# The masked cross-attention of a two-layer decoder, rewritten: strips, a ring of four, last keys a group ahead

## The chip, the cores and the metric

One core of one Trainium2 chip runs the whole program in one launch. The metric is the device time of that launch in microseconds (us), the median of several runs. The engines are PE (TensorE, matmuls; PEld its weight loads), DVE (VectorE), ACT (ScalarE), POOL (GpSimd) and SP (SyncE, which here only issues DMAs). Each takes its own instructions strictly in order and waits at semaphores for the others.

## What is computed

Six layers follow each other on x of 128 batches x 32 tokens x 256 features. The change lies in the first one, a cross-attention over 257 keys per batch with a mask:

```
x = x + L0_xattn(layernorm(x), ctx, ctx, mask, Wq, bq, Wk, bk, Wv, bv, Wo, bo)
   q, k, v: 16 heads of 16 features;  scores = q k^T / 4, masked keys at -1e9
   softmax over the 257 keys;  out = (probs v) Wo + bo
x = x + L0_attn(layernorm(x))      (state space)
x = x + L0_ffn(layernorm(x))       (quantised)
x = x + L1_xattn(layernorm(x), ctx, ctx)   (sigmoid in place of softmax, no mask)
x = x + L1_attn(layernorm(x));  x = x + L1_ffn(layernorm(x))   (experts)
```

## The kernel before, in words

Each layer is a function that is run to its end before the next starts. `cross_attention(..., layer=0)` makes the first; `soft` is true there. Nearly every product is made of three fp16 matmuls: an operand is kept as a high part (`kh`, `vh`, `pTh`, ...), which ACT rounds out of the fp32 result in PSUM, and a low part (`kl`, `vl`, `pTl`), which DVE gets by subtracting; `split_products` pairs high*high, high*low and low*high.

The work is cut into 128 batches, four to a group (128 tokens) and eight to a pass of the hardware loop. Each engine has its `body(i)` with a fixed order of steps for `c` in 0 to 7, written out by hand; nothing else sets the order. For batch b:

- PE: `keys` (12 matmuls of 256 columns into `psK`), `values` (12 into `psV`), `scores`: one product for each four of the 16 heads, 3 matmuls of 128 rows, 12 in all, into `psS`; right behind them the scores of the 257th key, 12 matmuls of one column, into `psSx`. Zeros in `qbd` (the queries spread to 8 heads of 32 tokens, others masked by `mask8`) keep heads apart. Two batches later `transposes` (8, fp32) turns the probabilities into `psT`, and `pv` multiplies them with the values into `psO`.
- DVE: `softmax_max` adds the mask to the 257th score (L842), then adds the mask to the scores and takes the row maximum, one instruction for each four heads (L847), then scales the maxima to the exponent's bias `nm` (L850). `recip` makes 1/sum. `lo_k`, `lo_v`, `lo_pT` make low parts. `extract` picks, out of `psO`, each head's own rows: one step on ACT and three on DVE (L907) for each pair of batches.
- ACT: `hi_k`, `hi_v`, `hi_pT`, and `probs`: four exponentials with their sums (L709), when `nm` is there.
- POOL: `split` makes the two parts of the context; `spread` builds `qbd` (four instructions of 1024 elements a group, L360); `norm` multiplies the probabilities with 1/sum, four instructions a batch (L380), and copies the 257th into `px`. PE's `transposes` wait for that (`p_norm`).
- Once a group, at `c % 4` = 0 to 3, `psA`, a part of the PSUM tile `psM`, is used in turn for the transposed x (`xnT`), the queries, the 257th keys and values (`row257`, with DVE's `lo_257` at L817 and L819 and `mask_257` at L826), and the output product. `psX` and `psSx`, other parts of `psM`, take the transposed 257th probabilities and the 257th scores.

K, `prob` and the maxima have two buffers, `pTh`/`pTl` one, V four. The fourth layer's `sigmoid_attention` (x1), which stays as it is, does a like job without softmax: four buffers for K, V and pT, keys two batches ahead, and matmuls that use parts of the array: two of 64 rows side by side in its `scores` (L1247), four of 32 columns side by side in its `attend` (L1267).

Of the kernel before, what the change touches and what calls it, by code (L numbers as in the profile page):

```python
# [180 lines left out]
def cross_attention(nc, d, xres, con, norm, layer):  # L181

    soft = layer == 0
    with ExitStack() as ctx:
# [1 line left out]
        sb, ps, sem = sp.sb, sp.ps, sp.sem  # L190
# [18 lines left out]
        V = [(sb(f"vh{n}", [P, C, 256], F16), sb(f"vl{n}", [P, C, 256], F16)) for n in range(4)]
        kx = [(sb(f"kxh{n}", [P, C, GB], F16), sb(f"kxl{n}", [P, C, GB], F16)) for n in range(2)]  # L210
        xk = (sb("xkh", [P, C, 96], F16), sb("xkl", [P, C, 96], F16))
        vx3 = sb("vx3", [96, D], F16)
        vxm = [sb(f"vxm{n}", [96, GB, D], F16) for n in range(2)]

        NP = 2
        prob = [sb(f"prob{n}", [P, 4, S2], F32) for n in range(NP)]
        pT32 = sb("pT32", [P, 4 * 256], F32) if not soft else None
        mx = [sb(f"mx{n}", [P, 4], F32) for n in range(2)]
        nm = [sb(f"nm{n}", [P, 4], F32) for n in range(2)]
        sm = [sb(f"sm{n}", [P, 4], F32) for n in range(2)]  # L220
        rs = [sb(f"rs{n}", [P, 4], F32) for n in range(2)]
        pT = [(sb(f"pTh{n}", [P, 2, 512], F16), sb(f"pTl{n}", [P, 2, 512], F16)) for n in range(1 if soft else 2)]
# [9 lines left out]
        psA = psM[:, 0:256]
        psX = psM[0:96, 256:384]
        psKx = psM[:, 384:392]
        psSx = psM[:, 392:408]
        score = [psS, psS] if soft else [psS, psT]
        SC = 0.25 / (WS * WS)
        PXS = 1.0 if soft else PS

        const_in, bias_ready, px_zeroed = sem("const_in"), sem("bias_ready"), sem("px_zeroed")  # L240
        ctx_in = [sem(f"ctx_in{n}") for n in range(2)]
        mask_in, mask_used = sem("mask_in"), sem("mask_used")
        pool_passed, sync_passed = sem("pool_passed"), sem("sync_passed")
# [3011 lines left out]
```

## Time and profile before

| | us |
|---|---|
| median of 3 runs | 3246.75 (3215.63 to 3252.71) |
| the profiled execution's own time | 3239.74 |
| its span, first to last instruction | 3237.9 |
| PE busy | 2671.7 (83%) |
| DVE busy | 2315.1 (71%) |
| ACT busy | 1925.8 (59%) |
| POOL busy | 1795.2 (55%) |

The median lies 7.0 us, 0.2%, above the profiled execution. The shares are means over six layers with different limits; the changed layer has the first 1130 us or so, and is to be read for itself. A busy engine is one with an instruction in it, and matmuls overlap, so what a matmul costs PE is the distance to the next start, not its duration.

### The profile page before, as it was taken

The page shows a single profiled execution, that of the slowest core. Times are in us where ns is not written, and L with a number is a line of the kernel's source. Part 1 is how long each engine was busy: PE and PEld are TensorE (multiplying, and loading weights), DVE is VectorE, ACT ScalarE, POOL GpSimd, SP SyncE. Part 2 cuts the span into 40 slices and gives each one's busy share as a digit, 9 for nine tenths or more (in the row PEclk, how much of TensorE's full clock was granted, in tenths as well). Part 3 has the DMA queues.
Part 4 walks back from the last instruction along what each step waited for, and adds up shares of the span by engine and source line. Part 5 has one row for each costly group of instructions (what it writes and reads, how often), then busy time and mean ns, then how long its engine had stood idle before and what let it go on. Part 6 is the DMA issues. An engine that isn't in the chain of part 4 may idle for free. (4 is left out here: it accounts for less than half of the span.)

```text
span 3237.9 us, 98846 instructions
## 1 busy us (share of the span) xinstructions
PE 2671.7 (83%) x35900; PEld 2137.6 (66%) x35901; DVE 2315.1 (71%) x5097; ACT 1925.8 (59%) x4544; POOL 1795.2 (55%) x2064
## 2 busy tenths in 40 slices
PE   3988888898888739999859699999994878537998
PEld 2777677777766627777635488888883667435776
DVE  4998899999888748888843577777775888563343
ACT  2666566666665548888724477777773656243333
POOL 4776777787776434555410466666662777133222
PEclk9999999999999859999979899999996999558999
DMA  4111111111110000000000222211110000351110
GB/s 142 41 59 41 44 56 49 48 59 39 42 59 28 14 1 1 1 0 0 1 28 1 77 60 70 61 58 58 59 44 16 2 2 2 133 193 49 36 34 28
DMA packets 87222, 140.66 MB, mean 43 GB/s; under 512 B 11040, under 2 KB 74304, under 8 KB 80736
## 3 DMA queue, kind: packets, MB, share of 16 engines
q1 hardware_dynamic: 82336, 123.04, 12.2%
q0 software_dynamic: 4672, 14.57, 1.3%
q8 instruction: 159, 2.61, 0.3%
q14 instruction: 55, 0.45, 0.0%
HBM read 122.88 MB, written 14.69 MB: 42 GB/s over the span
## 5 line engine op out<-in xcount | busy, mean ns | idle before, releaser
L380 POOL TENSOR_SCALAR x_prob<-x_prob,x_rs 128x257 f32<-128x257 f32 x512 | 246.8, 482 | 216.9 <-DVE x_rs L856 184.7
L709 ACT ACTIVATE x_prob<-x_prob,x_nm 128x257 f32<-128x257 f32 x512 | 254.4, 498 | 179.7 <-DVE x_nm L850 179.6
L2134 DVE TENSOR_TENSOR_SCAN m_s<-m_a,m_psBx 128x2048 f32<-128x2048 f32 x64 | 282.5, 4415 | 16.2 <-PE m_psBx L1909 15.7
L1425 DVE SCALAR_TENSOR_TENSOR x_pTl<-x_psS,x_pTh 128x1024 f16<-128x1024 f32 x128 | 156.8, 1225 | 168.0 <-ACT x_pTh L1333 168.0
L1920 PE MATMUL m_psS<-m_s,all_ident 128*128 128x256 f32 x1024 | 237.4, 386 | 0.9 <-DVE m_s L2134 0.9
L847 DVE CUSTOM_DVE_ANT_0 x_prob<-x_psS,x_masked,x_prob 128x256 f32<-128x256 f32 x512 | 217.5, 481 | 22.1 <-DVE x_prob L842 21.6
L1920 PEld LDWEIGHTS m_psS<-m_s,all_ident 128*128 128x128 f32 x1024 | 190.6, 191 | 45.8 <-issue 21.4
L2041 ACT ACTIVATE m_a<-m_dt,m_rate 128x248 f32<-128x248 f32 x512 | 205.6, 490 | 4.4 <-DVE m_s L2134 4.2
L3039 ACT ACTIVATE e1t_g<-e1t_psH,e1t_bias 128x128 f32<-128x128 f32 x312 | 88.9, 368 | 183.6 <-PE e1t_psH L2988 183.6
L693 ACT ACTIVATE x_kh<-x_psK,x_bk 128x256 f16<-128x256 f32 x256 | 107.3, 470 | 132.8 <-PE x_psK L265 130.2
L468 PE MATMUL x_psT<-all_ident,x_prob 128*128 128x128 f32 x1024 | 141.5, 282 | 52.4 <-issue 31.1
L865 DVE TENSOR_TENSOR x_pTl<-x_psT,x_pTh 128x512 f16<-128x512 f32 x256 | 164.1, 682 | 5.6 <-ACT x_pTh L680 2.9
L1114 POOL TENSOR_TENSOR x_qbdh<-x_qh,all_mask4h 128x1024 f16<-128x1024 f16 x32 | 60.6, 1893 | 176.7 <-DVE x_ql L1406 176.7
L468 PEld LDWEIGHTS x_psT<-all_ident,x_prob 128*128 128x128 f32 x1024 | 117.6, 145 | 58.6 <-issue 52.5
L1106 POOL TENSOR_TENSOR x_ctxl<-x_ctx,x_ctxh 128x512 f16<-128x512 f32 x128 | 148.6, 1161 | 10.7
L2988 PE MATMUL e1t_psH<-e1t_xnh,e_wh 128*128 128x128 f16 x624 | 143.4, 230 | 8.0 <-issue 7.5
L352 POOL TENSOR_TENSOR x_ctxl<-x_ctx,x_ctxh 128x512 f16<-128x512 f32 x128 | 143.4, 1120 | 10.7
L265 PE MATMUL x_psS<-x_kh,x_qbdh 128*128 128x256 f16 x512 | 142.4, 278 | 7.1 <-POOL x_qbdl L360 3.6
L1153 PE MATMUL x_psK<-x_ctxh,x_wkh 128*128 128x256 f16 x512 | 141.4, 276 | 4.7 <-POOL x_ctxl L1106 3.4
L1346 ACT ACTIVATE x_vh<-x_psV 128x512 f16<-128x512 f32 x128 | 76.4, 597 | 114.5 <-PE x_psV L1153 114.5
L265 PE MATMUL x_psV<-x_wvh,x_ctxh 128*128 128x256 f16 x512 | 143.4, 280 | 0.0
L265 PE MATMUL x_psV<-x_wvl,x_ctxh 128*128 128x256 f16 x512 | 143.2, 280 | 0.0
(554 smaller groups left out, 11481.1 us busy)
## 6 DMA issues: line engine op xcount, KB each, us to landing
x_ctx<-in_ctxT SPq DMA_DIRECT2D x32, 1028.0 KB, 5.3
x_ctx<-in_ctxT SPq DMA_DIRECT2D x32, 1024.0 KB, 6.0
x_mraw<-in_mask SPq DMA_DIRECT2D x128, 128.5 KB, 2.6
e1r_stage<-in_L_ffn_w SPq DMA_DIRECT2D x16, 1024.0 KB, 5.0
e_rows<-e1r_pad POOLq DMA_DIRECT2D x1, 5070.0 KB, 20.6
e1t_row<-e_rows SPq DMA_DIRECT2D x39, 130.0 KB, 2.1
all_xres<-in_x SPq DMA_DIRECT2D x1, 4096.0 KB, 14.4
x_vxr<-x_vx SPq DMA_DIRECT2D x128, 32.0 KB, 3.3
```

The source lines that it names most:

```text
L265: last = eng.matmul(out, a, b, start=start and n == 0, stop=stop and n == len(prods) - 1, skip_group_check=lint)
L352: pool.tensor_tensor(lo[:, j], src, hi[:, j], ALU.subtract).then_inc(ctx_split, 1)
L380: last = pool.tensor_scalar(prob[n][:, h, :], prob[n][:, h, :], rs[n][:, h:h + 1], PS, ALU.mult, ALU.mult)
L468: last = pe.transpose(psT[:, kt * 512 + h * P:kt * 512 + (h + 1) * P], prob[c % 2][:, h, kt * P:(kt + 1) * P], con["ident"][:])
L709: last = act.activation(prob[n][:, h, :], prob[n][:, h, :], ACT.Exp, bias=nm[n][:, h:h + 1], scale=SC, accum_out=sm[n][:, h:h + 1])
L847: dve.tensor_tensor_reduce(prob[n][:, h, 0:256], psS[:, h * 256:(h + 1) * 256], masked[gp][:, j, 0:256], 1.0, prob[n][:, h, 256:257], ALU. ...
L865: dve.tensor_tensor(pT[0][1][:, kt, :], psT[:, kt * 512:(kt + 1) * 512], pT[0][0][:, kt, :], ALU.subtract).then_inc(pt_lo, 1)
L1106: pool.tensor_tensor(lo[:, j], src, hi[:, j], ALU.subtract).then_inc(ctx_split, 1)
L1425: dve.scalar_tensor_tensor(pT[c % 4][1][:].rearrange("p r k n -> p (r k n)"), psS[c % 2][:], PS, pT[c % 4][0][:].rearrange("p r k n -> p ( ...
L1920: last = pe.matmul(psS[:, h * ST:(h + 1) * ST], con["ident"][:], S[h][:, :, m, :], start=m == 0, stop=m == NS - 1)
L2041: last = act.activation(A[h][:, :, m, 1:T], dt[c % 2][:, h, :].rearrange("p (b t) -> p b t", t=T)[:, :, 1:T], ACT.Exp, scale=rate[:, h, m: ...
L2134: dve.tensor_tensor_scan(rows(S), rows(A), psBx[:], 0.0, ALU.mult, ALU.add).then_inc(scan_done, 1)
```

## The change

`softmax_attention` takes the place of `cross_attention`; the other five layers are the same code.

- **Strips.** `scores` uses 64 rows of the array for four heads and the other 64 for the next four: per half 3 products, each as two matmuls side by side, into two different banks of `psS`. `qbd` is spread to 4 heads, not 8 (two POOL instructions a group). `attend` uses four strips of 32 columns side by side, 64 columns of data each.
- **Unnormalised weights.** POOL's `norm` is gone. The exponentials go straight to `transposes` (which wait for `exp_done`); the factor 4096 is applied where ACT and DVE take them out of `psT`. 1/sum is spread by POOL into `rsel` (`spread_sums`, 128 elements), turned to the layout of the output by two fp32 matmuls into `psR` (`attend_last`), and multiplied in by DVE's `extract`, now two steps on DVE.
- **The scale in the maximum.** L791 multiplies by `-SC` and takes the minimum, so that its result is the exponent's bias, and `probs` waits for each of the four results by itself.
- **A ring of four** for `prob`, `low` and K; two for pT. Keys two batches ahead, values one ahead; transposes one batch behind, attend two behind.
- **Last keys.** Keys and values of the 257th row for all 128 batches are made once at the start; the values go out to DRAM and come back in three copies for each group. Its scores are made for a whole group, a group ahead (`last_scores`, 24 matmuls of two columns), taken by DVE in one instruction (`take_scores`) and put into `prob` by POOL (`put_score`).
- **Order.** Each engine's `body` is new.

What it comes to on two engines, in the middle of a loop pass. DVE before, from one batch's low values to the next (L847: mask and maximum, its rows that repeat left out; `kxl` and `vx3` are the 257th row's, `oT` the output's own rows):

```order
L842 TENSOR_TENSOR x0_prob1<-x0_psM,x0_masked1 128x4 [waits x0_s_mm,x0_t_mm]
L847 ISA x0_prob1,x0_mx1<-x0_psS,x0_masked1,x0_prob1 128x256 [waits x0_sx_taken]
...
L850 TENSOR_SCALAR x0_nm1<-x0_mx1 128x4 [waits x0_s_max]
...
L886 SCALAR_TENSOR_TENSOR x0_kl0<-x0_psK,x0_bk,x0_kh0 128x256 [waits x0_s_mm,x0_k_hi]
...
L907 SCALAR_TENSOR_TENSOR x0_oT0<-x0_psO,all_mask4,x0_oT0 128x128 [waits x0_o_part]
...
L856 RECIPROCAL x0_rs1<-x0_sm1 128x4 [waits x0_p_main,x0_exp_done]
L817 SCALAR_TENSOR_TENSOR x0_kxl0<-x0_psM,x0_bk,x0_kxh0 128x4 [waits x0_vx_hi]
...
L819 TENSOR_TENSOR x0_vx3<-x0_psM,x0_vx3 32x256
...
L865 TENSOR_TENSOR x0_pTl0<-x0_psT,x0_pTh0 128x512 [waits x0_pv_mm,x0_pt_hi]
...
L894 TENSOR_TENSOR x0_vl2<-x0_psV,x0_vh2 128x512 [waits x0_pv_mm,x0_v_hi]
```

DVE now, the batch of a group in which most group steps fall (`obl`, `sxl`, once a group):

```order
L835 SCALAR_TENSOR_TENSOR x0_oT1<-x0_psO,all_mask2,x0_oT1 128x2x64 [waits x0_o_part]
L837 TENSOR_TENSOR x0_oT1<-x0_psO,x0_oT1 128x2x64 [waits x0_o_sum]
L791 ISA x0_prob2,x0_low2<-x0_psS,x0_masked0,x0_prob2 128x256 [waits x0_s_mm,x0_sx_put]
...
L820 SCALAR_TENSOR_TENSOR x0_kl0<-x0_psK,x0_bk,x0_kh0 128x256 [waits x0_s_mm,x0_k_hi]
...
L806 SCALAR_TENSOR_TENSOR x0_pTl1<-x0_psT,x0_pTh1 128x512 [waits x0_pv_mm,x0_pt_hi]
...
L798 RECIPROCAL x0_rs1<-x0_sm1 128x4 [waits x0_r_spread,x0_exp_done]
...
L843 SCALAR_TENSOR_TENSOR x0_obl0<-x0_oT1,x0_bv,x0_obh0 128x128 [waits x0_ob_hi]
...
L780 SCALAR_TENSOR_TENSOR x0_sxl1<-x0_psM,x0_barred1 128x16 [waits x0_sx_put]
L812 SCALAR_TENSOR_TENSOR x0_px3<-x0_psM,x0_px3 32x128 [waits x0_px_hi]
L828 TENSOR_TENSOR x0_vl3<-x0_psV,x0_vh3 128x512 [waits x0_pv_mm,x0_v_hi]
```

The 257th score's step and the scaling of the maxima have gone, `extract` stands ahead of the maxima and has one step less, the 257th row's `kxl` and `vx3` are replaced by one `sxl` for the whole group, and the low parts of the keys are those of two batches on.

PE before, the first matmul of each step of one batch (`psK` keys, `psT` transposes, `psV` values, `psS` scores, `psM` the 257th key's scores, `psO` the product with the values):

```order
L468 MATMUL x0_psT<-all_ident,x0_prob0 128x128 [waits x0_pt_lo,x0_p_norm]
...
L265 MATMUL x0_psV<-x0_wvh,x0_ctxh1 128x256 [waits x0_v_lo]
...
L265 MATMUL x0_psS<-x0_kh0,x0_qbdh1 128x256 [waits x0_s_max,x0_k_lo]
...
L265 MATMUL x0_psM<-x0_kxh1,x0_qbdh1 128x1 [waits x0_sx_taken]
...
L265 MATMUL x0_psK<-x0_ctxh1,x0_wkh 128x256 [waits x0_k_lo,x0_ctx_split]
...
L265 MATMUL x0_psO<-x0_pTh0,x0_vh0 64x128 [waits x0_pt_lo,x0_o_ext,x0_v_lo]
```

PE now, the same:

```order
L548 MATMUL x0_psS<-x0_kh1,x0_qbdh1 128x256 [waits x0_s_max,x0_k_lo]
...
L432 MATMUL x0_psK<-x0_ctxh1,x0_wkh 128x256 [waits x0_k_lo,x0_ctx_split]
...
L558 MATMUL x0_psT<-all_ident,x0_prob0 128x128 [waits x0_pt_lo,x0_exp_done]
...
L432 MATMUL x0_psV<-x0_wvh,x0_ctxh1 128x256 [waits x0_v_lo,x0_px_lo]
...
L574 MATMUL x0_psO<-x0_pTh1,x0_vh3 32x64 [waits x0_pt_lo,x0_v_lo]
...
L590 MATMUL x0_psO<-x0_px3,x0_vxm0 32x64 [waits x0_r_spread,x0_vxm_ready,x0_px_lo]
```

The transposes have moved from the head of the batch to behind the scores and the keys and wait for the exponentials, not for POOL; the single-column matmuls are gone from each batch; the last product now waits for POOL's `spread_sums` too.

The core of the diff (the order of each `body` is what the rows above show; DVE's and PE's lag by batch is as under **A ring of four**):

```
+            def put_score(i, c):
+                b, j, gp = i * 8 + c, c % GB, c // 4
+                wait_apart(pool, sx_taken, i * 2 + (gp + 1), pool_passed)
+                wait_apart(pool, t_mm, b - 3, pool_passed)
+                wait_apart(pool, px_put, b - 3, pool_passed)
+                pool.tensor_copy(prob[c % 4][:, :, LAST], sxl[gp][:, j, :]).then_inc(sx_put, 1)
...
-                    wait_apart(pool, r_ready, b + 1, pool_passed)
-                    for h in range(4):
-                        last = pool.tensor_scalar(prob[n][:, h, :], prob[n][:, h, :], rs[n][:, h:h + 1], PS,
-                                                  ALU.mult, ALU.mult)
-                    last.then_inc(p_main, 1)
...
+            def put_last(i, c):
+                b, j = i * 8 + c, c % GB
+                wait_apart(pool, exp_done, b * 4 + 4, pool_passed)
+                wait_apart(pool, pxT_mm, i * 4 + (c // 2 - 1), pool_passed)
+                dst = px[j // 2][:].rearrange("p (r z) -> p r z", r=3)[:, :, 4 * j:4 * j + 4]
+                pool.tensor_copy(dst, prob[c % 4][:, :, LAST].unsqueeze(1).to_broadcast([P, 3, 4])).then_inc(px_put, 1)
+
+            def spread_sums(i, c):
+                b, pair = i * 8 + c, c // 2 % 2
+                pool.wait_ge(r_ready, b + 1)
+                wait(pool, o_full, i * 4 + (c // 2 - 1))
+                pool.tensor_tensor(rsel[pair][:, c % 2], rs[c % 2][:].unsqueeze(2).to_broadcast([P, 4, T]),
+                                   token[:].unsqueeze(1).to_broadcast([P, 4, T]), ALU.mult).then_inc(r_spread, 1)
...
+            def last_scores(i, gp):
+                g = i * 2 + gp
+                pe.wait_ge(qbd_ready, g * 2 + 2)
+                for j in range(GB):
+                    for half in range(C):
...
+                wait(pe, s_max, b * 4)
+                for half in range(C):
+                    for m, (q, k) in enumerate(((0, 0), (0, 1), (1, 0))):
+                        for r in range(RG):
+                            rows = slice(64 * r, 64 * r + 64)
+                            to = r * 512 + half * LAST
+                            last = pe.matmul(psS[:, to:to + LAST], qbd[gp][q][rows, half, j].rearrange("p h q -> p (h q)"),
+                                             K[c % 4][k][rows, half, :], start=m == 0, stop=m == 2)
+                last.then_inc(s_mm, 1)
...
+                        to = (half * 2 + j % 2) * 64
+                        for v, p in ((0, 0), (0, 1), (1, 0)):
+                            for cg in range(4):
+                                frm = (half * 2 + cg // 2) * P + cg % 2 * 64
+                                last = pe.matmul(psO[32 * cg:32 * cg + 32, to:to + 64],
+                                                 V[c % 4][v][:, kt, half * P + 32 * cg:half * P + 32 * cg + 32],
+                                                 pT[c % 2][p][:, kt, frm:frm + 64],
+                                                 start=j % 2 == 0 and kt == 0 and half == 0 and (v, p) == (0, 0), stop=False,
...
+                for r in range(RG):
+                    last = pe.matmul(psR[64 * r:64 * r + 64].rearrange("p (c j t) -> p c j t", c=C, t=T), head_rows[:],
+                                     rsel[j0 // 2][:].rearrange("p j (c r) t -> p r c j t", c=C)[:, r],
+                                     start=True, stop=True, skip_group_check=True)
                 last.then_inc(o_full, 1)
...
+            def probs(i, c):
+                b = i * 8 + c
+                for h in range(4):
+                    act.wait_ge(s_max, b * 4 + h + 1)
+                    if h == 0:
+                        wait(act, r_ready, b - 1)
+                    act.activation(prob[c % 4][:, h, :], prob[c % 4][:, h, :], ACT.Exp, bias=low[c % 4][:, h:h + 1],
+                                   scale=-1.0, accum_out=sm[c % 2][:, h:h + 1]).then_inc(exp_done, 1)
...
-                wait_apart(dve, sx_taken, b + 1, dve_passed)
+                    wait_apart(dve, mask_used, i * 2 + (gp + 1), dve_passed)
                 for h in range(4):
-                    dve.tensor_tensor_reduce(prob[n][:, h, 0:256], psS[:, h * 256:(h + 1) * 256], masked[gp][:, j, 0:256],
-                                             1.0, prob[n][:, h, 256:257], ALU.add, ALU.max, mx[n][:, h:h + 1]).then_inc(s_max, 1)
-                dve.wait_ge(s_max, b * 4 + 4)
-                dve.tensor_scalar(nm[n][:], mx[n][:], -SC, None, ALU.mult).then_inc(nm_ready, 1)
+                    to = (h % 2) * 512 + (h // 2) * LAST
+                    dve.tensor_tensor_reduce(prob[c % 4][:, h, 0:LAST], psS[:, to:to + LAST], masked[gp][:, j, 0:LAST],
+                                             -SC, prob[c % 4][:, h, LAST:S2], ALU.add, ALU.min, low[c % 4][:, h:h + 1]).then_inc(s_max, 1)
...
+                dve.wait_ge(o_part, q + 1)
+                dve.scalar_tensor_tensor(dst, own_cols(1), con["mask2"][:, 1:2], dst, ALU.mult, ALU.add).then_inc(o_sum, 1)
+                dve.wait_ge(o_sum, q + 1)
+                dve.tensor_tensor(dst, psR.rearrange("p (c j t) -> p c j t", c=C, t=T), dst, ALU.mult).then_inc(o_ext, 1)
```

## Rows read from the trace of the kernel before

**Rows 1.** Busy time of each engine in three stretches (us, busy, instructions); clock, DMA.

```profile
300.00:600.00 300.00, 263.84 (x3374) 221.38 (x3373) 266.62 (x760) 192.72 (x598) 226.76 (x340) 0.98 0.17 53
...
1150.00:1200.00 50.00, 20.59 (x114) 14.08 (x114) 13.85 (x26) 21.14 (x39) 15.38 (x14) 0.57 0.00 0
...
2000.00:2400.00 400.00, 399.60 (x8694) 326.08 (x8692) 285.45 (x460) 300.63 (x480) 269.96 (x230) 1.00 0.21 62
```

**Rows 2.** Line L842, once a batch: min/median/max ns, first and last start.

```profile
L842 DVE TENSOR_TENSOR x_prob<-x_psM,x_masked x128: 145/154/167, 59.3 to 1108.6; 128x4 f32<-128x4 f32 x128
```

**Rows 3.** DVE's groups, 300 to 600 us: busy us, mean ns, idle before.

```profile
L847 DVE CUSTOM_DVE_ANT_0 x_prob<-x_psS,x_masked,x_prob 128x256 f32<-128x256 f32 x148 | 62.9, 481 | 7.1 <-DVE x_prob L842 7.1
...
L850 DVE TENSOR_SCALAR x_nm<-x_mx 128x4 f32<-128x4 f32 x37 | 35.1, 950 | 1.3
...
L907 DVE SCALAR_TENSOR_TENSOR x_oT<-x_psO,all_mask,x_oT 128x128 f32<-128x128 f32 x54 | 18.7, 346 | 1.3
...
L826 DVE TENSOR_TENSOR x_vxm<-x_vx,all_vmask 96x1024 f16<-96x1024 f16 x9 | 6.1, 677 | 0.0
L842 DVE TENSOR_TENSOR x_prob<-x_psM,x_masked 128x4 f32<-128x4 f32 x37 | 5.7, 154 | 1.4 <-PE x_psM L265 1.4
...
L819 DVE TENSOR_TENSOR x_vx<-x_psM,x_vx 32x256 f16<-32x256 f32 x9 | 3.7, 417 | 0.1
...
L817 DVE SCALAR_TENSOR_TENSOR x_kxl<-x_psM,x_bk,x_kxh 128x4 f16<-128x4 f32 x18 | 3.2, 218 | 3.5 <-ACT x_vx L673 3.5
```

**Rows 4.** The longest waits, 300 to 600 us: total, times, longest.

```profile
ACT x_prob L709 <- DVE x_nm L850: 55.7, 36, 2.2
POOL x_prob L380 <- DVE x_rs L856: 44.2, 23, 7.2
```

**Rows 5.** Line L850 over the layer.

```profile
L850 DVE TENSOR_SCALAR x_nm<-x_mx x128: 169/590/1616, 61.2 to 1110.5; 128x4 f32<-128x4 f32 x128
```

**Rows 6.** The order of time around one L850: start, us, engine.

```profile
604.96 3.75 POOL L360 TENSOR_TENSOR x_qbdl<-x_ql,all_mask 128x1024 f16<-128x1024 f16 x2
...
607.28 1.45 DVE L850 TENSOR_SCALAR x_nm<-x_mx 128x4 f32<-128x4 f32 x1
```

**Rows 7.** The order of time, PE matmuls of this layer.

```profile
603.68 0.16 PE L265 MATMUL x_psM<-x_kxl,x_qbdh 128*128 128x1 f16 x1
...
603.70 0.16 PE L265 MATMUL x_psM<-x_kxh,x_qbdl 128*128 128x1 f16 x1
...
603.73 0.27 PE L265 MATMUL x_psK<-x_ctxh,x_wkh 128*128 128x256 f16 x1
...
603.84 0.27 PE L265 MATMUL x_psK<-x_ctxl,x_wkh 128*128 128x256 f16 x1
...
605.32 0.23 PE L265 MATMUL x_psO<-x_pTh,x_vh 128*64 128x128 f16 x2
...
605.38 0.23 PE L265 MATMUL x_psO<-x_pTl,x_vh 128*64 128x128 f16 x2
```

**Rows 8.** The order of time, PE matmuls of the fourth layer, x1.

```profile
2102.01 0.20 PE L1267 MATMUL x_psO<-x_pTh,x_vl 128*32 128x64 f16 x4
2102.03 0.20 PE L1267 MATMUL x_psO<-x_pTh,x_vh 128*32 128x64 f16 x4
...
2104.57 0.22 PE L1247 MATMUL x_psS<-x_qbdl,x_kh 64*128 64x128 f16 x2
2104.63 0.22 PE L1247 MATMUL x_psS<-x_qbdh,x_kl 64*128 64x128 f16 x2
2104.78 0.28 PE L1153 MATMUL x_psK<-x_ctxh,x_wkh 128*128 128x256 f16 x1
```

**Rows 9.** POOL's costliest group, 300 to 600 us.

```profile
L380 POOL TENSOR_SCALAR x_prob<-x_prob,x_rs 128x257 f32<-128x257 f32 x148 | 71.3, 482 | 53.7 <-DVE x_rs L856 44.2
```

**Rows 10.** Two groups of layer x1, 2000 to 2400 us.

```profile
L1124 POOL TENSOR_TENSOR x_vxm<-x_vxr,x_own_head 64x1024 f16<-64x1024 f16 x21 | 45.5, 2166 | 0.0
...
L1451 DVE SCALAR_TENSOR_TENSOR x_obl<-x_oT,x_obh 128x256 f16<-128x256 f32 x20 | 12.7, 633 | 0.0
```

More of the change, by code:

```diff
@@ L209, in cross_attention @@
[L209 to L222, printed above, removed]
+        last32 = sb("last32", [P, C, NB], F32)
+        (lastp,), (kxp,), (kx,) = parts("last", [P, C, NB], 1), parts("kxp", [P, C, NB], 1), parts("kx", [P, C, NB, RG], 1)
@@ L232, in cross_attention @@
[L232 to L243, printed above, removed]
@@ L259, in cross_attention @@
         block = ctx.enter_context(nc.Block())
-        def mm_split(eng, out, lhs, rhs, start, stop, lint=False):
-            prods = [p for a, b in zip(lhs, rhs) for p in split_products(a, b)]
-            for n, (a, b) in enumerate(prods):
-                last = eng.matmul(out, a, b, start=start and n == 0, stop=stop and n == len(prods) - 1,
-                                  skip_group_check=lint)
-            return last
-        def both(pair, f):
-            return (f(pair[0]), f(pair[1]))
@@ L426, in _, with products, part @@
             run(pool, body)
-            norm(LASTI, 8)
+            spread_sums(LASTI, 6)
+            put_last(LASTI, 7)
+            spread_sums(LASTI, 7)
         @block.tensor
         def _(pe):
+            def products(out, lhs, rhs):
+                prods = [p for a, b in zip(lhs, rhs) for p in split_products(a, b)]
+                for m, (a, b) in enumerate(prods):
+                    last = pe.matmul(out, a, b, start=m == 0, stop=m == len(prods) - 1)
+                return last
+            def part(pair, f):
+                return (f(pair[0]), f(pair[1]))
@@ new lines, in keys @@
+            def keys(i, c):
+                b, j, gp = i * 8 + c, c % GB, c // 4
+                pe.wait_ge(ctx_split, b + 1)
+                if isinstance(i, int) and b == 0:
+                    pe.wait_ge(kx_lo, 1)
+                wait(pe, k_lo, b)
+                for h in range(C):
+                    last = products(psK[:, h * LAST:(h + 1) * LAST],
+                                    [part(W["k"], lambda w: w[:, cc, h * P:(h + 1) * P]) for cc in range(C)],
+                                    [part(ctxp[gp], lambda x: x[:, j, cc, :]) for cc in range(C)])
+                last.then_inc(k_mm, 1)
@@ new lines, in values @@
+            def values(i, c):
+                b, j, gp = i * 8 + c, c % GB, c // 4
+                if isinstance(i, int) and b == 0:
+                    pe.wait_ge(vx_lo, 1)
+                wait(pe, v_lo, b)
+                for kt in range(2):
+                    last = products(psV[:, kt * D:(kt + 1) * D],
+                                    [part(ctxp[gp], lambda x: x[:, j, cc, kt * P:(kt + 1) * P]) for cc in range(C)],
+                                    [part(W["v"], lambda w: w[:, cc, :]) for cc in range(C)])
+                last.then_inc(v_mm, 1)
@@ L647, in _ @@
+            transposes(LASTI, 7)
+            turn_taken(LASTI, 7)
+            turn_last(LASTI, 8)
+            attend(LASTI, 6)
+            attend(LASTI, 7)
+            attend_last(LASTI, 7)
             output(LASTI, 1)
@@ L779, in _ @@
+            hi_px(LASTI, 8)
+            extract(LASTI, 6)
             hi_ob(LASTI, 1)
```

864 lines of the change are left out of this document (396 added, 468 removed).

## The prediction

> **What bounds the kernel now.** I read the windows first, to get the layer by itself, then the line that runs once a batch, for the pitch, and then groups, waits and the order of time inside the layer. The changed layer gives a batch every (1108.6 - 59.3)/127 = 8.262 us [rows 2]; that pitch, 127 times, is what the change works on. From 300 to 600 us, 148 maxima of four a batch make 37 batches, one in 8.11 us [rows 3]. Divided by 37, the busy times there are PE 7.13, DVE 7.21, ACT 5.21, POOL 6.13 us a batch [rows 1]. So two engines are near the pitch at once, and each lacks about 0.9 to 1.0 us of being full. The waits say how that is lost: ACT waits 55.7 us for `nm`, and POOL 44.2 us for 1/sum [rows 4]. These lie on one loop: maxima on DVE, exponentials on ACT, 1/sum on DVE, scaling on POOL, transposes on PE, low parts on DVE again, with two buffers for `prob` and one for pT. ACT and POOL have slack; they are links of that loop, not limits by their own work. Neither PE nor DVE can be made faster alone.
>
> **PE, part by part**, by starts. A matmul of 256 columns starts 0.11 us after the last (603.73 to 603.84), one of a single column 0.025 (two between 603.68 and 603.73), a pair of the product with the values 0.06 [rows 7]. In layer x1 two matmuls of 64 rows and 128 columns start as a pair each 0.06 us, half of 0.11 for half the columns, so the second strip is free; and four strips of 32 columns and 64 data columns start each 0.03 us (2102.01 to 2102.03) [rows 8].
> - Scores: 12 x 0.11 = 1.32 before, 6 pairs x 0.11 = 0.66 now: -0.66.
> - Product with the values: 12 pairs x 0.057 = 0.68 before, 12 fours x 0.03 = 0.36 now: -0.32.
> - Single-column scores: 12 x 0.025 = 0.30 a batch before; 24 of two columns a group, 0.15 a batch: -0.15.
> - 257th keys and values once a group, 12 narrow and 6 wide matmuls, 0.30 + 0.66 = 0.96, /4: -0.24. They are made once at the start.
> - `attend_last`: 4 fours and two fp32 matmuls of 128 columns a pair of batches, in place of four of 128 columns (4 x 0.06). The fp32 ones cost between 0.1 and 0.3 us each; I take 0.2, so 0.12 + 0.4 - 0.24 = 0.28 a pair, +0.14.
> - Changes between whole and split array: in x1 the first whole matmul starts 0.15 us after the last pair (2104.63 to 2104.78), 0.09 more than the pitch [rows 8]. Scores go in and out once a batch: +0.18. The product with the values had its strips before.
> Sum: 7.13 - 0.66 - 0.32 - 0.15 - 0.24 + 0.14 + 0.18 = **6.08 us of PE a batch**. Keys, values and transposes are untouched and are most of it.
>
> **DVE.** Gone: `nm` 0.950; the 257th score 0.154; of three `extract` steps a pair one, 0.346/2 = 0.17; `mask_257` 0.677/4 = 0.17; `vx3` 0.417/4 = 0.10; `kxl` 2 x 0.218/4 = 0.11 [rows 3]. New: `sxl`, like the 0.154 row, 0.04; `lo_ob` now in two halves, each reading two SBUF tensors. The maxima still pitch as before (same shape, 481 ns). The nearest row to `lo_ob` is x1's 633 ns for both halves at once [rows 10]; two halves cost between that and twice it, against one instruction of about 0.42 (`vx3`, same columns): +0.05 to +0.21, I take 0.12. Sum: 7.21 - 1.65 + 0.16 = **5.72**.
>
> **ACT and POOL.** ACT loses the 257th row and half of `hi_ob`; it stays under its 5.21. POOL loses four scalings, 4 x 0.482 = 1.93 [rows 9], and two of four `spread` instructions of 3.75/2 = 1.88 each [rows 6], 0.94 a batch. It gains `own_rows`, near x1's 2.166, 0.54 a batch [rows 10], two small steps a batch of not over 0.2 each beyond the copy it had, and `spread_sums`, an eighth of a `spread` instruction, 0.25. Sum 6.13 - 1.93 - 0.94 + 0.54 + 0.65 = 4.4. Both lie well under PE. They cost nothing as work, but are links: what waits behind them is named under the rivals.
>
> **What is late next.** PE has the most work, 6.08, DVE 5.72 right under it. Of the loop, the links over POOL's scaling (four instructions, 1.9 us) and over `nm` are out; the first exponential may start after the first maximum. I walked one batch through the new orders, with t = 0 at DVE's first maximum of batch b. The maxima end at 1.65 and PE's scores of b+1 start (the one-deep `psS` waits for them). Keys of b+3 end about 3.9. The exponentials of b end near 2.2, low parts of b-1 near 3.9, so the transposes of b start without a wait. Values of b+2 follow by 5.7, when DVE's low values of b+1 are just done. The product of b-1 needs `extract`, the first thing in DVE's next turn. It fits, but with margins of some tenths only at `values`, `extract` and `psS`. DVE's turns are uneven: the one at `c % 4` = 0 carries the mask conversion and the queries. So I take 0.4 us of wait a batch on PE. Below it lies layer x1, same ring and lags, in which PE is busy 399.6 of 400 us, no wait [rows 1]; above it the 0.98 us of today. Pitch 6.08 + 0.42 = **6.50**.
>
> **The sum.** 127 x (8.262 - 6.50) = 223.8 us less. Start and end: four more constants are loaded ahead of the first context, the 257th rows of all batches go through PE once, and at the end one softmax tail without POOL's scaling; I take them together at 0, within 8 us either way. 3239.74 - 223.8 = 3016; the median shown lies 7 us above the profiled execution, so **3023 us**. What a measurement of this kernel can tell from no change is about 2%, 65 us, so faster means a pitch under about 7.75.
>
> **A rule against the trace.** L850 writes 4 numbers a row and takes 169 ns at best, 950 on the mean of the stretch [rows 3, 5]. In the order of time it starts at 607.28 and ends at 608.73, and POOL's `spread`, begun at 604.96, ends at 608.71 [rows 6]. So 0.78 of the 0.95 us taken off DVE above is waiting for POOL. The question is if the wait goes, or falls on DVE's next instruction.
>
> The Trainium skill, SBUF — State Buffer, "Who interferes with whom", says that DVE and GpSimd share a port pair as an exclusive lock, and that of DVE's instructions only 2-port forms such as `tensor_scalar`, and those with two SBUF inputs while GpSimd reads, are shut out. By this rule the wait goes with L850, since what follows reads PSUM; but `lo_ob` now has two SBUF inputs, twice a group. The trace agrees as far as it goes: x1's L1451, of that kind, has 633 ns.
>
> **Rivals.**
> 1. *No waits, as in x1.* For it: the same ring, and room on DVE. Against: x1 has no maximum and no transposes. Pitch 6.1 to 6.2: 3239.74 + 7 - 127 x 2.11 = 2979.
> 2. *The loop holds.* Today's 0.98 us of wait stays: `put_score` of a group waits for `take_scores`, which DVE does only behind `lo_ob` in the third batch; POOL's `spread` and `own_rows` delay `put_last`, for which PE's turn of `px` waits, and `spread_sums`, for which `attend_last` waits with the next scores and keys queued behind. Pitch 7.06: 3239.74 + 7 - 152.7 = 3094.
> 3. *The wait for POOL moves on.* 0.78 us falls on another DVE instruction: DVE 6.50, with 0.4 of waits 6.9: 3239.74 + 7 - 173 = 3074. POOL works less (4.4 for 6.13), which speaks against the whole of it.
> 4. *The strips do not run side by side here*, so that the change does not do what it says: scores 12 x 0.11 and the product with the values 48 x 0.03 = 1.44 cost 0.66 + 1.08 more, PE 7.82, pitch 8.2: 3239, no change. Rows of x1 speak against it.
> 5. *Slower: the clock.* Granted clock is 0.98 while PE is busy 264 of 300 us, and 0.57 while it is busy 20.6 of 50 [rows 1]. If the new waits let it fall to the lower of its levels (1.2 GHz) inside the layer, PE's 6.08 doubles to 12.2: 3247 + 127 x 3.9 = 3742. It decides from a mean clock under 6.08/8.26 = 0.74. But PE would be busy 6.08 of 6.5, more than today.
>
> **Chances.** Forecast (pitch 6.25 to 6.8) 0.50; rival 1 0.16; rivals 2 and 3 together 0.26, of which 0.02 beyond 7.75; rival 4 0.05; rival 5 0.03. That makes faster 0.90, within 2% 0.07, slower 0.03. The range has to take in rivals 1 to 3 with start and end: from 2979 less 8, rounded down to cover a cheaper `attend_last` (0.1 us a batch, 13 us), to 3094 plus 8 and a little for POOL's part: 2960 to 3115. Outside lie rivals 4 and 5 and the thin ends.
>
> **What the profile after would show.** Right: a pitch of 6.5; PE busy some 6.1 us a batch and over 90% of the layer, clock 0.98; score matmuls in pairs at 0.11 us; DVE near 5.7; the waits for `nm` and 1/sum gone, ACT idle for PE's keys and values. Wrong, by step: pairs at twice that start distance (rival 4); PE waiting on `px_put`, `r_spread` or DVE on `sx_put` for over 0.5 us a batch (rival 2); DVE rows such as the maxima or `lo_ob` longer than before (rival 3). The forecast fails most easily where my 0.4 us of wait is off, as it is a choice between rows, each 0.1 us being 13 us of the total.

## The result, and the profile after

The changed kernel takes 3121.8 us (median of 4 runs, 3112.6 to 3149.0) against 3237.6 in the same session, a ratio of 0.9675 [0.9593, 0.9757]. The forecast was 3023, the range 2960 to 3115. Line L791 has the maxima now, four a batch: the first at 58.1, the last at 944.0 us, so a pitch (the time from one batch to the next) of 885.9/127 = 6.98 us (before 8.262 [rows 2]; forecast 6.50).

Busy time of each engine in the profile after, as in [rows 1]; the short stretches are one passage between two passes of the layer's loop:

```profile
300.00:600.00 300.00, 268.08 (x4780) 222.27 (x4778) 241.81 (x744) 208.32 (x644) 180.01 (x268) 0.95 0.20 59
...
326.00:328.00 2.00, 2.00 (x77) 1.64 (x75) 2.00 (x6) 2.00 (x9) 2.00 (x3) 1.00 0.23 39
328.00:330.00 2.00, 0.45 (x15) 0.20 (x4) 1.23 (x3) 1.26 (x5) 1.92 (x4) 1.00 1.00 342
330.00:332.00 2.00, 0.00 (x0) 0.00 (x0) 0.29 (x1) 0.00 (x0) 2.00 (x7) 1.00 0.47 152
332.00:334.00 2.00, 0.10 (x2) 0.11 (x4) 0.00 (x0) 0.00 (x0) 1.68 (x2) 0.78 0.00 0
334.00:336.00 2.00, 2.00 (x16) 1.17 (x15) 0.12 (x1) 0.00 (x0) 0.00 (x0) 0.50 0.03 8
336.00:338.00 2.00, 2.00 (x11) 1.51 (x10) 1.58 (x8) 0.00 (x0) 0.00 (x0) 0.50 0.00 0
338.00:340.00 2.00, 2.00 (x13) 1.93 (x12) 0.87 (x2) 0.98 (x3) 0.00 (x0) 0.51 0.00 0
340.00:342.00 2.00, 2.00 (x34) 1.68 (x35) 1.42 (x3) 2.00 (x7) 0.00 (x0) 1.00 0.00 0
```

The first stretch holds 42 batches (x167 of L791): PE 6.38, DVE 5.76 busy a batch, pitch 7.14, where 6.08, 5.72 and 6.50 were forecast. The short ones show where it goes: TensorE stands for over 5 us, then works for 6 us at a granted clock of 0.50 (334 to 340 us), the lower of its two levels (1.2 GHz). The waits after, whole run for the first two, 300 to 600 us for the rest:

```profile
PE x_psS L548 <- issue: 69.0, 13, 5.5
PE x_psS L1190 <- issue: 34.1, 6, 5.7
...
ACT x_kh L680 <- PE x_psK L432: 82.9, 43, 8.9
POOL x_prob L350 <- DVE x_sxl L780: 56.1, 10, 5.6
POOL x_rsel L388 <- DVE x_rs L798: 45.9, 11, 8.6
...
DVE x_prob L791 <- PE x_psS L548: 27.4, 5, 5.6
...
ACT x_prob L664 <- DVE x_low L791: 7.0, 10, 0.8
```

Of the waits of [rows 4], ACT's for the bias has shrunk from 55.7 to 7.0 us. POOL still waits for 1/sum, 45.9 us for 44.2, but now with `spread_sums`, and no wait of TensorE for `rsel` appears in this stretch. At the top is a wait whose releaser is "issue": no semaphore explains it. It comes 13 times, each time before the first score matmul of a pass, and the layer's loop jumps back 13 times (of its 16 passes, the first and the last are written out, 14 are in the loop). In x1, whose code the change leaves alone, it comes 6 times. The order of time on PE around one of them:

```profile
328.01 0.44 PE L594 MATMUL x_psO<-x_rsel,x_head_rows 128*64 128x128 f32 x4
333.90 0.40 PE L548 MATMUL x_psS<-x_kh,x_qbdh 64*128 64x256 f16 x2 [5.45 <-issue]
334.08 0.42 PE L548 MATMUL x_psS<-x_kl,x_qbdh 64*128 64x256 f16 x2
```

Two more rows are of the kernel before, the same waits in the whole run and x1's line L1425; the last is the latter's counterpart after, L1368:

```profile
PE x_psT L468 <- issue: 31.1, 10, 4.7
...
L1425 DVE SCALAR_TENSOR_TENSOR x_pTl<-x_psS,x_pTh x128: 1223/1225/1226, 1835.0 to 2440.4; 128x1024 f16<-128x1024 f32 x128
```

```profile
L1368 DVE SCALAR_TENSOR_TENSOR x_pTl<-x_psS,x_pTh x128: 1223/1225/1226, 1663.6 to 2316.0; 128x1024 f16<-128x1024 f32 x128
```

x1 took 605.4 us and takes 652.4. From here on "x0" and "x1" are the times from first to last start of DVE's `x_pTl` in the two layers; x0 fell from 1041.4 to 878.9 (69.3 to 948.2), 162 us, of which x1 gives 47 back. They and the stalls are those of the one profiled execution of each kernel, the times in the tables the medians of all.

### The profile page after: what moved, and what is told of

The parts are those of the page before. It is cut to its first block and busy times, and to the rows that moved or that the text cites. A ratio compares the mean times of both kernels' runs of the same rounds, so it can differ in the third digit from the quotient of the medians.

```text
span 3122.1 us, 105389 instructions
## 1 busy us (share of the span) xinstructions
PE 2561.8 (82%) x38670; PEld 2034.0 (65%) x38671; DVE 2130.9 (68%) x4719; ACT 1878.5 (60%) x4388; POOL 1542.9 (49%) x1680
## 5 line engine op out<-in xcount | busy, mean ns | idle before, releaser
L1368 DVE SCALAR_TENSOR_TENSOR x_pTl<-x_psS,x_pTh 128x1024 f16<-128x1024 f32 x128 | 156.8, 1225 | 206.8 <-ACT x_pTh L1276 206.8
L791 DVE CUSTOM_DVE_ANT_0 x_prob<-x_psS,x_masked,x_prob 128x256 f32<-128x256 f32 x512 | 216.6, 478 | 73.5 <-PE x_psS L548 71.7
L664 ACT ACTIVATE x_prob<-x_prob,x_low 128x257 f32<-128x257 f32 x512 | 253.5, 503 | 20.6 <-DVE x_low L791 20.6
L806 DVE SCALAR_TENSOR_TENSOR x_pTl<-x_psT,x_pTh 128x512 f16<-128x512 f32 x256 | 163.5, 679 | 4.9 <-ACT x_pTh L672 4.0
L1270 ACT ACTIVATE x_psS<-x_psS 128x1024 f32<-128x1024 f32 x128 | 129.0, 1008 | 59.7 <-PE x_psS L1190 57.3
L1049 POOL TENSOR_TENSOR x_ctxl<-x_ctx,x_ctxh 128x512 f16<-128x512 f32 x128 | 149.5, 1168 | 10.7
L337 POOL TENSOR_TENSOR x_ctxl<-x_ctx,x_ctxh 128x512 f16<-128x512 f32 x128 | 148.9, 1163 | 10.7
L432 PE MATMUL x_psK<-x_ctxh,x_wkh 128*128 128x256 f16 x512 | 148.3, 290 | 5.8 <-POOL x_ctxl L337 3.4
L1096 PE MATMUL x_psK<-x_ctxh,x_wkh 128*128 128x256 f16 x512 | 144.3, 282 | 4.5 <-POOL x_ctxl L1049 3.0
L432 PE MATMUL x_psK<-x_ctxh,x_wkl 128*128 128x256 f16 x512 | 147.8, 289 | 0.0
L432 PE MATMUL x_psK<-x_ctxl,x_wkh 128*128 128x256 f16 x512 | 147.8, 289 | 0.0
L672 ACT ACTIVATE x_pTh<-x_psT 128x512 f16<-128x512 f32 x256 | 138.9, 594 | 12.0 <-PE x_psT L558 9.2
L1096 PE MATMUL x_psK<-x_ctxl,x_wkh 128*128 128x256 f16 x512 | 143.3, 280 | 0.0
```

The costliest lines, as they stand in the source:

```text
L337: pool.tensor_tensor(lo[:, j], src, hi[:, j], ALU.subtract).then_inc(ctx_split, 1)
L432: last = pe.matmul(out, a, b, start=m == 0, stop=m == len(prods) - 1)
L664: act.activation(prob[c % 4][:, h, :], prob[c % 4][:, h, :], ACT.Exp, bias=low[c % 4][:, h:h + 1], scale=-1.0, accum_out=sm[c % 2][:, h:h ...
L791: dve.tensor_tensor_reduce(prob[c % 4][:, h, 0:LAST], psS[:, to:to + LAST], masked[gp][:, j, 0:LAST], -SC, prob[c % 4][:, h, LAST:S2], ALU ...
L806: dve.scalar_tensor_tensor(pT[c % 2][1][:, kt, :], psT[:, kt * 512:(kt + 1) * 512], PS, pT[c % 2][0][:, kt, :], ALU.mult, ALU.subtract).th ...
L1049: pool.tensor_tensor(lo[:, j], src, hi[:, j], ALU.subtract).then_inc(ctx_split, 1)
```

## The experiments

Every instruction of TensorE between two branches was counted in the built programs, a matmul as two (weight load and product). x0's loop is 1526 instructions long before and 1892 after, x1's 1683 in both.

| kernel | us | ratio | x0 | x1 | issue stalls at pass heads, x0 / x1 |
|---|---|---|---|---|---|
| after | 3121.8 | 0.968 | 878.9 | 652.4 | 13 (69.0 us) / 6 (34.1) |
| a_flat0 | 3044.1 | 0.948 | 748.3 | 707.4 | 0 / 13 (74.7) |
| a_flat01 | 2935.7 | 0.914 | 750.8 | 607.8 | 0 / 0 |
| b_flat0 | 3210.3 | 1.000 | 1002.3 | 605.8 | 0 / 0 |
| a_pad64 | 3189.5 | 0.991 | 893.0 | 717.3 | 13 (90.3) / 13 pairs (75.2) |
| a_late | 3101.9 | 0.961 | 845.5 | 695.3 | 13 (43.7) / 11 (63.0) |
| a_thin | 3017.9 | 0.938 | 759.7 | 664.7 | 0 / 7 (40.6) |
| f_thin | 2923.1 | 0.908 | 734.6 | 607.7 | 0 / 0 |
| f_all | 2919.4 | 0.907 | 747.4 | 608.8 | 0 / 0 |
| a_pad32 | 3194.7 | 0.992 | 892.7 | 707.9 | 13 (91.2) / 13 (74.1) |
| a_pad96 | 3069.0 | 0.953 | 879.2 | 606.8 | 13 (68.3) / 0 |
| b_long | 3378.0 | 1.049 | 1076.0 | 705.8 | 13 (41.7) / 13 (73.8) |
| f_dve | 2972.9 | 0.922 | 783.4 | 609.5 | 0 / 0 |

A stall is here an idle time of TensorE at the head of a pass that the profile puts down to "issue". Theory: TensorE's jump back to a loop's head has to bring code in again. First rival: a wait that the trace fails to name.

**a_flat0, a_flat01, b_flat0.** `run(pe, body)` replaced, on TensorE alone, in x0 or in x0 and x1:

```
-            run(pe, body)
+            for turn_i in range(LASTI + 1):
+                body(turn_i)
```

> The changed kernel, with TensorE's passes of the changed layer written out one behind the other (16 bodies, no loop on this engine; the other engines keep theirs). Theory: the 13 idle stretches of about 5.3 us that the profile after puts down to issue (69.0 us together) are TensorE's jump back to the head of its loop, whose code has to be brought in again. Written out, there is no jump: no issue row for L548 is left, and the half-rate matmuls behind each stall (x_psS and x_psK in 391.75 to 394.4 at 0.213 us apart instead of 0.107, some 1.3 us a pass, 17 us in all) go too. 3122 - 69 - 17 = 3036 us if nothing else is late next, up to 3060 if VectorE (5.76 us busy a batch) takes some back. x1 keeps its stalls (about 6 of 13 passes). Rival, a wait that the trace fails to name (a semaphore from another engine at the start of each pass): the stall stays where it is, with a straight program too, and the time stays within 15 us of 3122.

> As a_flat0, and TensorE's loop in x1 (the same attention in the second half of the network, whose code the change doesn't touch) is written out as well. Theory: x1's 6 stalls (34.1 us in the profile after, none before) are the same thing, brought about because the code ahead of x1 got longer, and x1's stretch of 652.4 us goes back to the 605.4 us that it took before: 47 us more than a_flat0, 2990 to 3015 us. Rival, the changed layer leaves something behind that slows x1 (clock, data placement in SBUF): x1 stays at about 650 us.

> The kernel before, with TensorE's passes of the layer x0 written out. Its profile shows 31.1 us of issue idle before L468 in 5 of 13 passes. Theory: these go, and some us of half-rate matmuls behind them: 3238 - 31 - 5 = about 3200 us. What is left is then what the change is worth without any stall: a_flat0 against b_flat0 in x0's own stretch. Rival (those stalls are hidden by VectorE, which is 7.21 us busy a batch of 8.26): 3230 to 3240 us.

The stalls vanish with the jumps, and x1 goes back to its old length with its own jumps gone: the semaphores are all still there, so the rival is out, and the changed layer leaves nothing behind that slows x1 (607.8 us for 605.4 before). The gain in x0 is more than expected, 128 us in a_flat01 for 69 of standing. One thing came otherwise: in a_flat0 I had expected x1 to keep its 6 stalls; it has 13 and takes 707.4 us, which ate some 55 us of the gain. Its code lies further back there. In a_flat01, the same stretch of time and VectorE's costliest group:

```profile
300.00:600.00 300.00, 291.90 (x5763) 245.43 (x5762) 291.59 (x898) 249.08 (x772) 213.18 (x317) 1.00 0.25 70
```

```profile
L792 DVE CUSTOM_DVE_ANT_0 x_prob<-x_psS,x_masked,x_prob 128x256 f32<-128x256 f32 x204 | 86.4, 479 | 2.6 <-issue 2.0
```

51 batches, PE and DVE 5.72 us busy each, pitch 5.88, clock 1.00. Of 9.8 us that a jump costs x0 (128/13), 5.3 are standing. Work of 6 us at half clock is work of 3 at the full one, so I put 3 more down to the clock (an estimate). Some 1.5 are left; that they are the refilling of the chain of engines is not shown. b_flat0's x0 is 39 us shorter than in the profile before, as expected, but its time is that of the kernel before (0.9999 [0.9977, 1.0021]), whose runs of that session go from 3198.6 to 3245.9, where b_flat0's stay within 3209.3 to 3212.3. How many stalls the faster of those runs had no profile shows. Jumps out of both, the change takes x0 from 1002.3 to 748.3, 254 us: more than the 224 forecast.

**a_pad64, a_pad32, a_pad96.** N matmuls without use (64, 32, 96) where TensorE waits 41 us for its first data. All of its code behind them lies 2N instructions later; the length of the loops and their order stay:

```
+            for _ in range(N):
+                pe.matmul(psX[0:4, 0:4], con["mask4h"][:], con["mask4h"][:], start=True, stop=True)
             last_keys()
```

> The changed kernel with 64 matmuls of 4x4 without use (128 instructions of TensorE, each matmul being a weight load and a product) ahead of its first real one, where TensorE stands idle for 41 us anyway. No loop's length or order changes, only where its code lies. The instruction queue moves 16 KB at a time, which is 256 instructions of 64 bytes; by my count x1's loop (1683 instructions) lay from block 42.56 to 49.13 before and lies from 46.69 to 53.27 now; here from 47.19 to 53.77; x0's loop (1892 instructions) from 7.27 to 14.66 instead of 6.77 to 14.16. Theory of placement: a loop that touches fewer blocks fits, so x1's stalls go (6 to 0, 47 us) and x0's 13 fall to some: 2990 to 3075 us. Rival, the length of the loop alone decides: x0 keeps 13 stalls of 5.3 us and x1 its 6, 3122 us. Second rival, a dependency: the same.

> As a_pad64, with 32 matmuls of 4x4 ahead of the first one instead of 64: all of TensorE's code lies 64 instructions (a quarter of a 16 KB block) later than in the kernel after. So far, by place: shift 0 gave 13 stalls of 5.3 us in x0 and 6 in x1; shift 128 gave 13 of 6.9 us in x0 and 13 pairs (3.9 + 1.8 us) in x1. Theory, the length of 1892 instructions is too much at any place and the place only sets how many blocks are late behind a jump: x0 keeps 13 stalls of 5 to 7 us, x1 has between 6 and 13: 3110 to 3190 us. Rival, the place can free x0: fewer than 13 stalls in x0, below 3080 us.

> The same with 96 matmuls ahead: all code 192 instructions later. The same theory gives 13 stalls in x0 and 3110 to 3190 us, since four places a quarter of a block apart then cover the whole block; the rival, that one of the places frees x0, fewer than 13 stalls and under 3080 us.

With the same work and order the time lies between 3195 and 3069 us, by where the code lies. x0 stalls 13 times at all four places, as expected, 5.3 us each at shift 0 and 192, 7.0 at 64 and 128. For x1 the place decides; with its stalls gone, a_pad96 lies below the 3110 to 3190 us expected, although x0 keeps all of its own. By my count its loop begins at 0.69 of a block of 256 instructions after (6 stalls), at 0.94, 0.19 and 0.44 in the three (13, 13, 0), at 0.56 before (0), 0.69 in a_late and a_thin (11, 7), 0.06 in b_long (13), and with 13 x 1892 instructions more ahead of it near 0.8 in a_flat0 (13): free around 0.5, bad around 0. For a_pad64 I had expected the opposite; I had taken block borders to lie where my count starts. b_flat0 (0.09, no stall) does not fit; there the count runs over 23,500 instructions and may be off. So it is shown that the place matters, and the rule for which place is good stays open.

**a_late.**

```
-                wait_apart(sync, ctx_split, (g - 1) * GB, sync_passed)
+                wait_apart(sync, ctx_split, (g - 1) * GB + 2, sync_passed)
```

> The changed kernel, where SyncE starts each later load of context (1 MB, 5.5 us from issue to landing) in the changed layer two batches later than now: its wait on ctx_split is (g-1)*4+2 instead of (g-1)*4. TensorE's code and its place are as in the kernel after. In the profile after, the load of 326.12 moves 366 to 391 GB/s from about 328.2 to 331.7, just where TensorE stands still from 328.45 to 333.90, and the instruction queue has its packets there. Theory A: the jump back brings in code again, and its packets stand behind the load on the same 16 DMA engines; with the load elsewhere each of x0's 13 stalls shrinks from 5.3 us to 2 to 3 us, 30 to 50 us less in all, and less time at half clock behind it: 3060 to 3095 us. Theory B: a fetch takes its 5 us whatever else the engines carry: 13 stalls of 5.3 us, 3122 us. Rival against both: the later load is late for its own group, waits of POOL for ctx_in appear, and the time rises over 3130 us.

The DMA view of the kernel after, 324 to 342 us, in slices of 0.45 us, has a context load right in the gap:

```profile
GB/s 0 0 0 0 0 0 0 48 143 230 366 391 382 385 310 112 0 0 0 0 0 0 36 0 0 0 0 0 0 0 0 0 0 0 0 0 0 0 0 0
...
q8 instruction: 2, 0.03, 0.7%
...
x_ctx<-in_ctxT SPq DMA_DIRECT2D x1, 1024.0 KB, 5.5
```

In a_late the same view, 318 to 332 us in slices of 0.35, holds a stall from 321.6 to 325.0 with nothing beside it but the instruction queue's two packets, the second as TensorE starts again; the load comes behind:

```profile
GB/s 0 0 0 0 0 0 0 0 0 0 0 0 47 0 0 0 0 0 0 0 47 0 0 0 0 0 0 0 0 18 79 111 275 366 386 380 383 351 369 252
...
q8 instruction: 2, 0.03, 0.9%
```

The stalls are as many as before the edit, 3.36 us long on the mean instead of 5.3, and x0 is 33 us shorter, nearly as theory A had it (2 to 3 us); 3.4 us is what stays with no load beside it. The stretch at clock 0.50 behind the stall is shorter too, about 3 us (325 to 328) for 6. In the whole time little of this is seen: 3101.9 us lies above the 3060 to 3095 expected, and its runs go from 3081 to 3131. The profile is of the longest of them and has 11 stalls in x1, from code at the same place that gave 6. So a loop can stall in more or fewer passes with its code at one place; what decides it there is not shown.

**a_thin, f_thin.** In `attend`:

```
-                        for v, p in ((0, 0), (0, 1), (1, 0)):
+                        for v, p in ((0, 0),):
```

> The changed kernel with attend's products hi x lo and lo x hi left out (16 matmuls a batch instead of 48), so that part of the computation is missing. TensorE's loop of x0 becomes 1380 instructions long instead of 1892 (before: 1526, with 2.2 packets of 16 KB a pass on the instruction queue where 6.0 would be a whole pass; after: about 9 where 7.4 would be a whole pass). Theory: a loop of that length stays, so the 13 stalls of x0 are gone without writing anything out, and its pitch is that of a_flat0, 5.9 us a batch against 6.97: x0 is some 135 us shorter, x1 takes 605 to 710 us by where it comes to lie; 2940 to 3045 us. Rival (a jump stalls at any length, what saved the kernel before was luck): stalls remain in x0, pitch above 6.6, over 3075 us.

> a_thin with TensorE's passes of x0 and x1 written out as in a_flat01; the same products are left out. It tells whether TensorE's own work still matters once the jumps are gone. In a_flat01 VectorE is busy 291.6 of 300 us and TensorE 291.9, in 51 batches: 5.72 us a batch each, of a pitch of 5.88. Theory, VectorE is the bound (my 5.72 us a batch): 32 matmuls a batch fewer change x0's pitch by less than 0.1 us, 2925 to 2936 us. Rival, TensorE is the bound: 32 x 8 ns or so a batch (groups of four start 0.03 us apart) are 0.25 us a batch less, 32 us, 2904 us.

The products high*low and low*high with the values are left out, so the result is not that of the layer. A loop of 1380 instructions does not stall, although it still jumps back 13 times: x0 is 759.7 us long. The instruction queue from 300 to 600 us moved nothing at all in a_thin (its list of queues has no q8 row) and this in f_thin, a_flat01, b_flat0, after and before, in this order (packets, MB, share of the DMA engines):

```profile
q8 instruction: 34, 0.56, 0.8%
```

```profile
q8 instruction: 46, 0.75, 1.1%
```

```profile
q8 instruction: 28, 0.46, 0.7%
```

```profile
q8 instruction: 47, 0.77, 1.0%
```

```profile
q8 instruction: 10, 0.16, 0.2%
```

That is 16 KB a packet. If a packet holds 256 instructions, straight code needs length/256 packets a pass: 1380/256 in 6.4 passes is 34.7, 1892/256 in 6.4 is 47.1, 1526/256 in 4.75 is 28.3; 34, 46 and 28 moved, without a stall. So what costs is not bringing code in but a jump to code that isn't there. The loop after brings more than its whole length each pass (47 in 5.25 passes, 9.0 for 7.4); the loop before kept most of it (2.2 of 6.0); 1380 instructions stay entirely. Once jumps are gone, taking these matmuls off TensorE (f_thin) gives 16 us in x0, half of the 32 that the rival had and a little more than the 13 that the theory allowed.

The Trainium skill, Runtime: NRT & Kernel Launch, "Instruction fetch mechanics", gives TensorE room for 2048 instructions, refilled in blocks of 256, and says that prefetch goes straight on and that a taken branch whose target is not in the current window of two pages has to wait for a fetch. The runs agree on the block (the packet counts above) and on the branch (13 stalls for 13 jumps, none without). They do not agree on two pages: a_thin's jump goes back over 1380 instructions, more than five blocks, and stalled in none of 13 passes; the measurement decides. Nor does a loop under 2048 instructions stay by its length alone: 1892 stalled at all four places tried.

**f_all.** `run(pe, body)` written out in all seven loops.

> The changed kernel with all seven loops of TensorE written out. a_flat01 left issue rows of 7.4 and 2.2 us (e1t_psH, e1t_psY) in the last layer, 2.0 and 1.2 us elsewhere, and these are rows inside passes as well as at their heads. Theory: little is left to take, 2920 to 2936 us. Rival: straight code has to be brought in all the time (51 batches of a_flat01 in 300 us brought 46 packets of 16 KB), and where a layer's TensorE code runs fast with nothing ahead it falls behind: over 2950 us.

2919.4 us (2917.8 to 2920.8), ratio 0.907 [0.902, 0.911], the fastest version that computes everything, as the theory had it. Against a_flat01's time that is 16 us less; x0 and x1 are about as long as there, and the gain lies behind x1.

**b_long.** In the scores of the kernel before, ahead of the products:

```
+                for _ in range(24):
+                    pe.matmul(out[0:4, 0:4], W["q"][0][:, 0, 0:4], W["q"][0][:, 0, 0:4], start=True, stop=True)
```

> The kernel before with 24 matmuls of 4x4 (x_psS<-x_wqh) added to each batch's scores, whose results the scores overwrite, so that TensorE's loop of x0 is 1910 instructions long instead of 1526. Theory: with the length of the loop of after it gets the stalls of after: an issue row of about 13 stalls and 50 to 90 us at the pass heads of x0 (before: 31.1 us in 10 pieces), and about 9 packets a pass on the instruction queue instead of 2.2. The matmuls cost something of their own: at 0.03 to 0.06 us each 0.7 to 1.4 us a batch, of which TensorE had 0.9 us to spare; together 3280 to 3480 us. Rival, the stalls of after come from something else in its code than the length: issue stays at 10 pieces and about 31 us.

At 1910 instructions the old layer stalls at all 13 jumps too (before: in 5), 3.2 us each, with 8.8 packets a pass (39 in 4.4 passes); no load lies in the gap that I looked at (324 to 326 us: 0 GB/s). So the length brings the stalls in the old layer too. But their 41.7 us lie below the 50 to 90 expected, and x0 grew by only 35 us, added matmuls included. Of the 138 us between the two profiled executions, 100 are x1's: 13 stalls, with its own code unchanged and only its place moved. Without them the time would have been near 3278, just under the range.

**f_dve.** a_flat01 with VectorE's `x_vl` done twice in x0.

```
+                dve.tensor_tensor(again[c % 4][:], psV[:], flat(V[c % 4][0]), ALU.subtract)
                 dve.tensor_tensor(flat(V[c % 4][1]), psV[:], flat(V[c % 4][0]), ALU.subtract).then_inc(v_lo, 1)
```

> a_flat01 with VectorE's x_vl instruction (685 ns) given twice a batch in x0, the second result to a tile that nobody reads. Theory, with the jumps gone VectorE sets x0's pitch, as my sum of 5.72 us had it: the layer gets 128 x 0.685 = 88 us longer, 3015 to 3024 us. Rival, TensorE or a chain of waits sets it and VectorE has room: less than 40 us more, under 2976 us.

x0 grew 33 us, not 88, so the theory is out. Rows of f_dve:

```profile
300.00:600.00 300.00, 283.48 (x5459) 233.47 (x5460) 295.29 (x905) 238.78 (x735) 202.44 (x300) 1.00 0.23 66
```

```profile
L774 DVE TENSOR_SCALAR x_masked<-x_mraw 128x1028 f32<-128x1028 int32 x12 | 12.6, 1053 | 0.0
```

VectorE is busy 98% and per batch (48.75) only 0.34 us more. The mask conversion takes 1053 ns here, 1650 in a_flat01, 1155 before; and durations overlap (a_flat01's groups sum to 332.7 us for 291.6 busy), so 685 ns is not what an instruction takes off a full engine. In a_flat01 VectorE and TensorE are about equally full, with 0.16 us a batch to spare each, and neither sets the pitch alone: less work on the one gave 0.13 us a batch (f_thin), more on the other cost 0.26.

## Why the prediction was wrong

**The step that failed is "What is late next"**, in two places: the waits ("0.4 us of wait a batch on PE", semaphores only) and the boundary, which held the other five layers unchanged. The cost of a jump back to code that is no longer there was put at nothing, and a longer body on TensorE brings it at every jump. That puts 1.01 us a batch on x0's pitch (878.9 against 750.8 us in a_flat01, over 127 batches: 6.92 against 5.91), and 47 us on x1. Against the forecast: 127 x (6.98 - 6.50) = 60 us and 47 us, 107; 3023 + 107 = 3130 for the 3121.8 measured. The row of the cause stood in the profile before, 31.1 us of "issue" in ten pieces, and I priced neither it nor what more instructions a pass would do to it.

**The miss is small by luck.** Without jumps the pitch is 5.91, 0.59 under my 6.50; 75 us too much for work and waits hid more than half of the 128 that the jumps cost x0. With a right pitch for a layer without jumps the forecast would have been 2948, and the miss 174 us.

**PE, 6.08: too high.** Without jumps it is 5.72. The single terms hold in a_flat01: score pairs start 0.11 us apart, fours 0.03, and the first score pair starts 0.15 behind the last four. The two fp32 matmuls of `attend_last`, for which my 0.2 us each had no row behind it, take 0.37 together; the whole step puts 0.57 on a pair of batches (0.72 from the last four to the next scores, where without it 0.15 pass), for my 0.52. So the base, 7.13 of busy time, carried some that was no work; b_flat0 has 7.04, and the other 0.3 us stay open.

**DVE, 5.72: right**, 5.72 in a_flat01 and 5.76 after, but some of it by offsetting: the two halves of `lo_ob` take 334 ns each, +0.06 a batch where I took 0.12, and the mask conversion got longer by 0.12, which I did not have. ACT (4.96, forecast under 5.21) and POOL (4.29 for 4.4) are right.

**Rival 1 was the nearest for the layer itself**: without jumps 0.16 us a batch of TensorE is idle, and the pitch lies even below its 6.1. **Rival 2** would have given 3094, near the measured time, for a wrong reason: in the kernel after, TensorE waits for `put_last` once, 2.2 us. But with the jumps out, its link is what is left. Over the whole of a_flat01 (total, times, longest):

```profile
PE x_psM L472 <- POOL x_px L382: 20.4, 29, 3.6
```

That is 0.16 us a batch. **Rival 3**: the wait for POOL went with L850, but 0.5 us a group, 0.12 a batch, fell on the mask conversion (L772, 1155 ns before, 1651 after), a `tensor_scalar`, the form that the rule weighed ahead names. The trace agrees: one at 345.17 us ends at 346.82, 0.55 behind the end of POOL's L358 (344.37 to 346.27), and the shortest takes 686 ns in all. **Rival 4** is out: strips run in pairs and fours. **Rival 5** showed in small: the clock halves for 6 us of work behind each stall, 0.37 us a batch in the loop by the estimate above.

## What to carry to other kernels

Count a loop body's instructions on each engine before and after an edit: on TensorE 1380 stayed loaded, 1526 nearly, 1683 by its place, and 1892 never. A jump that stalled cost 10 us in x0 (128/13), about half of it behind the stall, and 8 in x1 (47/6). Where a profile shows "issue" at the first instruction of a pass, try the loop written out on that engine, or a shorter one, and look at the unchanged layers too, since code that moves can stall where it did not before.

## What was unexpected of the hardware

64 idle instructions at the head of the program changed its time from 3122 to 3195 us, 192 to 3069. The standing behind a jump was 3.4 us, 5.3 with a 1 MB load beside it, 7.0 with the code at another place and a load beside it too. Kernels in which a loop stalls in some passes only spread over 36 to 47 us within a session (after, 4 runs; before, 15), those with x0's and x1's or all loops written out over 2 to 9.
